# Metaformer block on one core: biases on a one in the input, moved tiles straight to the score rows, the opening re-ordered

## The reference, cut to what matters

```python
t = layernorm(x) @ W_prep + b_prep            # W_prep: 64 x (5*8*32): q_n, q, k, k_m, v
# wins: 32 windows, 64 tokens, 8 heads, 32 channels
bias, pat_n, pat_m = spatial(intrinsic)       # by relative position, 64 x 8 x 64 (x 32)
score = bias + einsum('bhod,ohid->bohi', q_n, pat_n)
score = score + einsum('bhod,bhid->bohi', q, k)
score = score + einsum('bhid,ohid->bohi', k_m, pat_m)
score = (score - mean_i) / std_i
x = x + einsum('bohi,bhid->bohd', score, v) @ W_fin + b_fin
x = x + experts(layernorm(x))                 # router, top 2 of 8, GELU, 64 -> 256 -> 64
```

## Time and profile before

| | |
|---|---|
| runs | 205.88 us median, 204.19 to 206.62 |
| profiled execution | 203.32 us, span of instructions 201.5 us |
| TensorE busy | 174.9 us (87%) |
| VectorE, ScalarE, GpSimd busy | 108.1, 117.9, 85.9 us |
| granted TensorE clock | 0.975 of full in the mean |
| DMA | 10868 packets, 12.96 MB |
| chain that ended last | TensorE 67%, GpSimd 14%, VectorE 8%, DMA 3% |

### The profile page before, as it was taken

One profiled execution on the slowest core, in us unless ns is written; L12 is line 12 of the kernel. 1 busy time (PEld: TensorE's weight loads), 2 busy tenths in 40 slices (PEclk: granted clock), 3 DMA queues, 4 the chain that ended last, 5 costly groups with the idle time before them and its releaser, 6 DMA issues.

```text
span 201.5 us, 4321 instructions
## 1 busy us (share of the span) xinstructions
PE 174.9 (87%) x1582; PEld 108.6 (54%) x1582; DVE 108.1 (54%) x296; ACT 117.9 (59%) x233; POOL 85.9 (43%) x130
## 2 busy tenths in 40 slices
PE   0519999999998799936995999999999999999983
PEld 0417554654555575626854856575556665655531
DVE  1594258445546525207386955196928773874323
ACT  2244397446453798808596497546666566676730
POOL 6120549040001999993866638481910073031000
PEclk9999999999999999985999789999999999999999
DMA  6930276969991002000300000000000000000000
GB/s 146 245 119 0 90 239 210 335 163 220 220 218 23 0 3 88 20 0 3 102 5 0 2 5 0 0 0 0 3 26 0 0 3 28 0 2 0 29 0 26
DMA packets 10868, 12.96 MB, mean 64 GB/s; under 512 B 2512, under 2 KB 8216, under 8 KB 10848
## 3 DMA queue, kind: packets, MB, share of 16 engines
q1 hardware_dynamic: 9936, 11.73, 22.2%
q10 hardware_dynamic: 528, 0.85, 1.5%
q0 software_dynamic: 384, 0.11, 0.5%
HBM read 7.94 MB, written 4.75 MB: 63 GB/s over the span
## 4 chain that ended last, share of the span: by engine, by line
PE 67%; POOL 14%; DVE 8%; DMA 3%; issue 3%; ACT 3%; SPq 1%; DVEq 0%; ACTq 0%; POOLq 0%
PE PS L731 13%; POOL SCN L437 10%; PE PS L571 9%; PE PS L719 7%; PE PS L720 6%; PE PS L805 4%; PE PS L585 4%; PE PS L780 4%; PE PS L595 3%; DMA XR<-in_x 3%; POOL RSC L455 3%; PE PS L628 2%; PE PS L604 2%; PE PS L769 2%; PE PS L698 1%
## 5 line engine op out<-in xcount | busy, mean ns | idle before, releaser
L938 ACT ACTIVATE HR<-PS,B1P 128x512 f32<-128x512 f32 x64 | 39.0, 693 | 5.0 <-PE PS L720 4.9
L731 PE MATMUL PS<-HR,W2s 128*64 128x512 f32 x128 | 31.0, 605 | 0.0
L437 POOL TENSOR_TENSOR SCN<-SCN,TMS 128x512 f32<-128x512 f32 x16 | 19.7, 1284 | 21.7 <-DVE SCN L1099 21.7
L719 PE MATMUL PS<-X,W1H 128*128 128x512 f32 x64 | 27.5, 430 | 0.0
L720 PE MATMUL PS<-X,W1L 128*128 128x512 f32 x64 | 25.8, 404 | 0.0
L443 POOL COPY PW<-PG 128x512 f32<-128x512 f32 x16 | 10.4, 684 | 34.1 <-DVE PG L1187 33.9
L1019 ACT ACTIVATE GB<-PS 128x512 f32<-128x512 f32 x16 | 9.6, 598 | 23.0 <-PE PS L805 23.0
L455 POOL TENSOR_TENSOR RSC<-VB,NHALF 128x32 f32<-128x32 f32 x4 | 21.9, 5463 | 0.3
L1158 DVE TENSOR_TENSOR SR<-PS,SCN 128x512 f32<-128x512 f32 x16 | 10.7, 685 | 13.6 <-PE PS L684 11.5
L974 ACT ACTIVATE BV<-PS 64x256 f32<-64x256 f32 x32 | 12.2, 380 | 7.6 <-PE PS L669 7.3
L731 PEld LDWEIGHTS PS<-HR,W2s 128*64 128x64 f32 x128 | 7.8, 136 | 13.3 <-issue 12.3
(11 more groups left out here) (149 smaller groups left out, 321.8 us busy)
## 6 DMA issues: line engine op xcount, KB each, us to landing
moved<-TMG SPq DMA_DIRECT2D x16, 256.0 KB, 2.9
TMS<-moved SPq DMA_DIRECT2D x16, 256.0 KB, 8.0
W1R<-in_W SPq DMA_DIRECT2D x4, 256.0 KB, 4.0
XR<-in_x SPq DMA_DIRECT2D x4, 128.0 KB, 4.7
W1E<-in_W SPq DMA_DIRECT2D x2, 256.0 KB, 6.2
W2s<-in_W SPq DMA_DIRECT2D x1, 512.0 KB, 3.7
out<-XR SPq DMA_DIRECT2D x4, 128.0 KB, 1.8
REL<-in_rel ACTq DMA_DIRECT2D x2, 225.0 KB, 5.1
```

The costliest lines, as they stand in the source:

```text
L437: G.tensor_tensor(pair, pair, TMS[:, t, :], ALU.add).then_inc(scn_ready, 1)
L719: nc.tensor.matmul(ps[:, :], W1H[:, col:col + P], X2[:, j * 512:j * 512 + 512], start=True, stop=False)
L731: m = nc.tensor.matmul(ps[d * C:d * C + C, :], W2s[:, 2 * (2 * ep + d) + c, :], HR[(4 * u + 2 * c + d) % 8][:, :], start=(c == 0), stop=(c ...
L938: A(HR[n % 8][:, :], PS[b][:, :], ACT.Gelu, bias=B1P[:, col:col + 1]).then_inc(bank_drained[b], 1)
```

## The change

- **Biases.** XF is stored as the transposed input plus one. The weights are centred over the 64 channels by a product with CEN (so that the one adds nothing), and b / 64 is added to each channel's weight by a first product of IDN with BPS (so that the one adds b; the normalised input sums to zero over channels). `bias_terms`, BI, YB, the DRAM tensor `bias_rows` and its DMAs go. The relative bias is added to the n table by SEL, with RB now on 4 x 2 rows in four DMAs.
- **Tiles of the m table.** SP sends each tile from TMG straight into SCN: two DMAs a tile, each with 128 source rows of 256 values and four target partitions, 32 in all. `moved`, TMS and GpSimd's additions go. VectorE adds the turned tiles of the n table to SCN in place, after a wait for all 32.
- **Order.** The n table is made before the transposes of XN. After the m tiles come all the keys and centred values, the experts' bias, and then the n tiles with their turned tiles alone. Keys and XC copies have no bias and are shared by ScalarE and VectorE. XN: two groups on VectorE, one on ScalarE, one on GpSimd. TensorE's first product waits for CEN and BPS, both from GpSimd. SP loads x 0, x 1, the weights and patterns; ScalarE's queue has b_prep, x 2 and x 3.
- **Buffers.** SQ has the place of TMS, and the opening's small tensors lie in it; TAM too.

The diff, cut:

```diff
-    plan += [(("xt", j), (4, 5, 7, 6)[j], 1) for j in range(NG)] + [(("wb",), 0, 1)]
+    plan += [(("tn", h), (4, 5, 7, 6)[h], 1) for h in range(4)]
+    plan += [(("xt", j), j, 1) for j in range(NG)]
     for m in range(8):
-        plan += [(("m", 2 * m + r), 4 + 2 * (m % 2) + r, 1) for r in range(2)]
-        if m == 1:
-            plan += [(("tn", h), h, 1) for h in range(4)]
+        plan += [(("m", 2 * m + r), 2 * (m % 2) + r, 1) for r in range(2)]
         if m == 3:
-            plan += [(("a", h), h, 1) for h in range(4)]
+            plan += [(("a", h), 4 + h, 1) for h in range(4)]
+    for m in range(8):
+        plan += [(("yk", 2 * m + r), 4 + 2 * (m % 2) + r, 1) for r in range(2)]
+        if m % 2 == 1:
+            plan += [(("xc", m // 2), m // 2, 1)]
+    plan += [(("b1", r), 4 + r, 1) for r in range(2)]
     for m in range(9):
         if m < 8:
-            plan += [(("n", 2 * m + r), r, 1) for r in range(2)]
-            plan += [(("yk", 2 * m + r), 4 + r, 1) for r in range(2)]
+            plan += [(("n", 2 * m + r), 4 * (m % 2) + r, 1) for r in range(2)]
         if m >= 1:
-            plan += [(("s", 2 * m - 2 + r), 2 + r, 1) for r in range(2)]
-        if m < 8 and m % 2 == 0:
-            plan += [(("xc", m // 2), 6, 1)]
-        if m == 1:
-            plan += [(("b1", r), 6 + r, 1) for r in range(2)]
...
-            for j in range(NG):
+            for j in range(2):
                 sp.dma_start(XR[:, 4 * j:4 * j + 4, :], x[:, 4 * j:4 * j + 4, :]).then_inc(x_in[j], 16)
-            sp.dma_start(BP[:, :], b_prep).then_inc(bp_in, 16)
-            sp.dma_start(B1[:, :], b1).then_inc(b1_in, 16)
+            sp.dma_start(WS[:, :], W_prep[:, 0:V * 256]).then_inc(wprep_in, 16)
+            sp.dma_start(REL[:, 1, :, :], rel[:, 1, :, :]).then_inc(relm_in, 16)
+            sp.dma_start(REL[:, 0, :, :], rel[:, 0, :, :]).then_inc(reln_in, 16)
+            for r in range(2):
+                sp.dma_start(WV[C * r:C * r + C, :], W_prep[:, V * 256:]).then_inc(wv_in, 16)
             for r in range(2):
...
             for tile in range(16):
                 sp.wait_ge(*drained("m", tile))
-                sp.dma_start(moved[P * tile:P * tile + P, :], TMG[:, tile, :]).then_inc(moved_out, 16)
-                if tile == 7:
-                    sp.wait_ge(bias_out, 16)
-                    load_bias(sp, 1)
-            sp.wait_ge(moved_out, 16 * 16)
-            rows = moved.rearrange("(i w) f -> i w f", w=NW)
-            for k in range(NPAIR // 2):
                 for g in range(2):
-                    sp.dma_start(TMS[C * g:C * g + C, 2 * k:2 * k + 2, :].rearrange("p t (b f) -> p (t b) f", b=2),
-                                 rows[:, 4 * k:4 * k + 4, 256 * g:256 * g + 256]).then_inc(moved_in[k], 16)
+                    tokens = SCN[C * g + 4 * tile:C * g + 4 * tile + 4, :, :, :, :]
+                    sp.dma_start(tokens.rearrange("p t b h o -> p (t b) (h o)"),
+                                 TMG[:, tile, 256 * g:256 * g + 256]).then_inc(moved_in, 16)
 
             sp.wait_ge(*filled("score", NPAIR // 2 - 1))
...
-            pool.dma_start(RB[:, :], rel0).then_inc(rel0_in, 16)
+            for h in range(4):
+                pool.dma_start(RB[HD * h:HD * h + 2, :], rel0.rearrange("(g h) r -> h g r", g=2)[h])\
+                    .then_inc(rel0_in, 16)
             for r in range(2):
                 pool.dma_start(LNB[C * r:C * r + C, :], ln_b).then_inc(lnb_in, 16)
...
+            G = nc.gpsimd
+            pool.wait_ge(consts_ready, 1)
...
+            pool.wait_ge(bp_in, 16)
+            G.tensor_scalar(BPS[:, :], BP[:, 0:SLOT], 1.0 / C, None, ALU.mult).then_inc(bps_ready, 1)
+            step(G.tensor_tensor(S2[:, :], IDN[:, 0:2], IDN[:, HD:HD + 2], ALU.add))
+            for h in range(2, 4):
+                step(G.tensor_tensor(S2[:, :], S2[:, :], IDN[:, HD * h:HD * h + 2], ALU.add))
+            G.tensor_scalar(SEL[:, :, :], S2[:, :].unsqueeze(2).to_broadcast([P, 2, P]), 1.0 / C, None,
+                            ALU.mult).then_inc(sel_ready, 1)
+            step(pool.memset(NHALF[:, :], -0.5))
+            pool.wait_ge(rx_ready, 1)
+            for q in range(12, NPAIR):
+                last = G.tensor_scalar(XN[:, q, :, :], twice(XR[:, q, :]), RS[:, q:q + 1], NB[:, q:q + 1],
+                                       ALU.mult, ALU.add)
+            last.then_inc(xn3_ready, 1)
...
-            pool.wait_ge(*drained("s", 14))
-            pool.wait_ge(*drained("s", 15))
-            for t in range(NPAIR):
-                if t % 2 == 0:
-                    pool.wait_ge(moved_in[t // 2], 32)
-                pair = SCN[:, t, :, :, :].rearrange("p b h o -> p (b h o)")
-                G.tensor_tensor(pair, pair, TMS[:, t, :], ALU.add).then_inc(scn_ready, 1)
 
...
+            def weights():
+
+                ps = begin("wt")
+                nc.tensor.matmul(ps[:, :], IDN[:, :], BPS[:, :].unsqueeze(2).to_broadcast([P, SLOT, C]),
+                                 start=True, stop=False)
+                for n_ in range(SLOT):
+                    m = nc.tensor.matmul(ps[:, n_ * C:n_ * C + C], WS[:, n_ * P:n_ * P + P], CEN[0:C, 0:C],
+                                         start=False, stop=(n_ == SLOT - 1))
+                end(m, "wt")
...
-            pe.wait_ge(consts_ready, 1)
+            pe.wait_ge(consts_ready, 2)
+            pe.wait_ge(bps_ready, 1)
             pe.wait_ge(wprep_in, 16)
...
+            weights()
             pe.wait_ge(relm_in, 16)
             pe.wait_ge(*drained("wt"))
             table("tm")
+            pe.wait_ge(reln_in, 16)
+            pe.wait_ge(rel0_in, 16 * 4)
+            pe.wait_ge(sel_ready, 1)
+            table("tn")
...
             for m in range(8):
                 pattern("m", m)
-                if m == 1:
-                    table("tn")
                 if m == 3:
                     products()
             for h in range(4):
+                pe.wait_ge(*drained("a", h))
+            for m in range(8):
+                mixed_keys(m)
+                if m % 2 == 1:
+                    centred(m // 2)
+            pe.wait_ge(w1e_in, 32)
+            pe.wait_ge(lnb_in, 32)
+            shift_bias()
+            for h in range(4):
                 pe.wait_ge(*drained("tn", h))
-                pe.wait_ge(*drained("a", h))
             for m in range(9):
                 if m < 8:
                     pattern("n", m)
-                    mixed_keys(m)
                 if m >= 1:
                     turned(2 * m - 2)
                     turned(2 * m - 1)
-                if m < 8 and m % 2 == 0:
-                    centred(m // 2)
-                if m == 1:
-                    pe.wait_ge(w1e_in, 32)
-                    pe.wait_ge(lnb_in, 32)
-                    shift_bias()
 
             def values(t):
                 ps = begin("v", t)
@@ -832,21 +788,19 @@
 
...
+                A(XF[:, 8 * j:8 * j + 8, :].rearrange("p w o -> p (w o)"), PS[b][:, :], ACT.Copy,
+                  bias=1.0).then_inc(bank_drained[b], 1)
...
+            dve.wait_ge(moved_in, N_MOVED)
+            for tile in range(16):
+                b = before[("s", tile)][0]
+                dve.wait_ge(*filled("s", tile))
+                part = SCN[:, :, :, :, 4 * tile:4 * tile + 4].rearrange("p t b h u -> p (t b) h u")
+                V_.tensor_tensor(part, PS[b][:, :].rearrange("p (h u w) -> p w h u", h=4, u=4), part,
+                                 ALU.add).then_inc(bank_drained[b], 1)
+            dve.wait_ge(*drained("s", 14))
+            dve.wait_ge(*drained("s", 15))
```

More of the change, by code:

```diff
@@ L202, in metaformer_kernel @@
         TMG = sb("TMG", [P, 16, 512])
[L204 to L219, removed]
+        WS = sb("WS", [C, 1024], at=sq_at)
+        WT_ = sb("WT_", [P, 4, 2, 2, C], at=sq_at)
+        REL = sb("REL", [P, 2, 2, NREL], at=sq_at)
+        RB = sb("RB", [P, NREL], at=sq_at)
+        TAM = sb("TAM", [P, SLOT, SIDE, SIDE], at=sq_at)
+        BPS = sb("BPS", [P, SLOT], at=sq_at)
+        VE = sb("VE", [P, NPAIR], at=sq_at)
+        RS = sb("RS", [P, NPAIR], at=sq_at)
+        RA = sb("RA", [P, NPAIR], at=sq_at)
+        BNX = sb("BNX", [P, NPAIR, 6], at=sq_at)
+        WARM = sb("WARM", [P, 1], at=sq_at)
+        NB = sb("NB", [P, NPAIR], at=sq_at)
+        assert sq_at[0] <= y_at[0]
+        PW = nc.alloc_sbuf_tensor_at("PW", [P, 4, 4, 2, C], F32, offset=scn_at[0])
         OR = sb("OR", [P, 8, 4, 2, HD + 1], at=late)
@@ L272, in metaformer_kernel @@
         small_in = sem("small_in")
[L273 to L276, removed]
+        moved_in = sem("moved_in")
         w1r_in = sem("w1r_in")
@@ L309, in metaformer_kernel, with twice @@
         N_SMALL = 9
[L311 to L315, removed]
-                queue.dma_start(BI[r0:r0 + WH, :, :], scratch[4 * g:4 * g + 4, :, lo:lo + WT]
-                                .rearrange("h j o -> j h o")).then_inc(bias_in[g], 16)
+        N_MOVED = 16 * 32
+        def twice(x):
```

(36 more changed lines are left out.)

157 lines of the change are left out of this document (39 added, 118 removed).

## The result

The changed kernel took 238.36 us in the median of four runs (236.47 to 241.26), the kernel before 206.25 on the same chip (204.19 to 208.25, four runs): ratio 1.151, 95% interval 1.134 to 1.167. It is slower, as forecast, but the forecast was 325 us; the profiled 236.47 us lie on the low end of the stated range (236), next to the third rival (246), which had set that end. Executions of one kernel can fall into two groups some 2 or 3% apart, so all ratios compare only the faster group of each kernel. The span of the profiled execution was 234.7 us.

A forecast was written before the change was run, and what follows sets the result against it. TensorE was taken to bound the kernel nearly throughout, with one break at GpSimd's 16 additions. Transfers done at 178.9 us, then 12.7, 3.4 for half clock and 130.4 after the last addition gave 325 us; range 236 to 341.

The forecast's parts named there:

- the third rival: Transfers to SCN: four engines drift apart to different partition groups, 55 GB/s, 76 us, 246 us in all; chance 0.25.
- The failed step: Transfers to SCN: priced from the bias_rows store out of eight partitions, 27 GB/s, 155 us for all 32.
- the 2.2 around a transfer: Transfers to SCN: 2.2 us added to their 155 us, from 2.9 to landing less 0.7 of moving.
- The argument used against drifting: Transfers to SCN: loads into 64 partitions also alternated between halves and stayed at 220 GB/s, so alternating didn't help.
- The rest of the sum: Whole kernel apart from moving the tiles: time is 170 us plus the transfers, once they outlast the cover.
- The opening: From the start to the m tiles: these begin at 19.7 instead of 21.26 us, a gain of 1.6 us.
- the 8.4 us expected from leaving out GpSimd's additions: Score stage: 6.4 us from an earlier RSC without TensorE's wait, plus 2.0 us from no half clock.
- no stall at RSC: Score stage: TensorE no longer waits at RSC, which ends at 84.1 instead of 90.8 us.
- the cover: TensorE work from the first transfer's issue at 21.7 to about 45 us, 23 us that can hide the transfers.
- the first: Rival for the transfers: several target groups fill at once, all hidden under 23 us, 191.6 us in all; chance 0.08.
- the second: Rival for the transfers: four engines each at full pace, 95 GB/s, 44 us, 214 us in all; chance 0.10.
- the fourth: Rival for the transfers: speed in proportion to partitions, 13.8 GB/s, 305 us, 475 us in all; chance 0.03.

The follow-up runs named there:

- m1: Only transfers of the changed kernel's shape, block not computed, in five series: 25 GB/s to one group of four partitions, 89 to 96 to partitions four apart.
- e1: Changed kernel with each transfer writing four partitions that lie four apart, in different groups; 225.22 us, ratio 1.121.
- e7: As e6, with the experts' bias products between the keys and the banks of the turned tiles exchanged; 216.76 us, ratio 1.057.
- e2: Changed kernel with the 32 transfers issued from GpSimd's queue instead of SP's; 249.01 us, ratio 1.238.
- e3: Changed kernel with the m tiles stored to DRAM and loaded back into SCN with 64 target partitions; 211.11 us, ratio 1.040.
- e5: Changed kernel with transfers from GpSimd's queue, each to four partitions of different groups; 216.08 us, ratio 1.045.
- e6: Changed kernel with transfers to four partitions of different groups, half issued by SP and half by GpSimd; 216.06 us, ratio 1.047.
- e8: Changed kernel with e7's two repairs and tiles over DRAM in two halves, loaded back by GpSimd's then SP's queue; 205.63 us beside 206.84 before.
- e9: As e8, with the DRAM tensor laid out so that loads read 8 KB rows and stores write 1 KB pieces; 207.92 us, ratio 1.016.
- e4: Changed kernel without the 32 transfers, SCN zeroed by GpSimd, so scores lack the m term; 199.9 us, ratio 0.974.
- f1: Kernel before, with SP sending the m tiles directly into TMS and nothing else changed; 247.71 us beside 206.84.
- f2: As f1, but GpSimd issues all loads of BI; 239.81 us, ratio 1.173.

## Why the prediction was right in its sign and wrong in its size

**The failed step** is the one that chose 27 GB/s, 155 us, for the transfers. The price itself was right for one group (25 measured, 26 at the start of the stretch), with some luck: it was read from a store to DRAM out of eight partitions, issued by GpSimd, and no run shows that the two have the same limit. To hold it for all 32 transfers was wrong. First issue to the end of the wait took 63.8 us, 61.6 without the 2.2 around a transfer: 68 GB/s in the mean. The engines drifted apart over different groups (m1, and the end packets in the changed kernel's own trace), and where nothing is shared the same shape has its full rate at once (e1). The argument used against drifting, that the loads into 64 partitions had alternated between halves and stayed at 220 GB/s, spoke about transfers with all 16 engines busy, each at 13.8 GB/s; it says nothing of four engines at one group, which have room to spread. Rival 3 had the mechanism, but took the loads' 13.8 GB/s for each drifted engine, 55 GB/s and 76 us; measured were up to 90, 22.5 an engine. That the time lies within the stated range is owed to this rival and not to the forecast's own step.

**The rest of the sum** was good to 5 us: 170.4 + 61.6 = 232.0 against 236.5. The difference, term by term:

- First issue at 23.05 instead of 21.7: +1.35. The first product started at 6.82 (6.9 forecast), but the weights took 5.7 us, not 3.6: the two passes of 512 columns took 2.04 us together, where I had 605 ns for one, and the 16 for centring 3.7 us, 0.23 us each and not 0.134. The opening gained 0.1 us.
- From the wait's end to the last addition 15.0 us, not 16.1: -1.1. The half clock after the wait was there.
- After the last addition 236.5 - 101.8 = 134.7 us, not 130.4: +4.3. Of the 8.4 us expected from leaving out GpSimd's additions 4.1 came. From the last addition to TensorE's first product after RSC it is 23.2 us, where before it was 92.25 - 64.5 = 27.75: 4.6 us and not 6.4, mostly since SR gained 0.7 us, not 2.0 (the bank, which e7 shows). The half clock behind the stall did go (1.00 from 125 to 132 us). But a later one grew: 0.51 for 7.0 us from 144 us on, behind 9 us in which TensorE was busy for 6.6, against this in the kernel before:

```profile
113.45:116.90 3.45, 3.45 (x16) 2.62 (x12) 2.26 (x8) 2.01 (x4) 0.63 (x1) 0.51 0.01 2
```

  That gives back 1.8 us, which leaves 0.7 of the 4.3 without a source. What sets the clock down there is open.

**Right:** the wait decides and stands ahead of the SCN additions; four engines; TensorE idle and then at half clock; no stall at RSC; the cover too short. **The rivals:** the first fell, and with it the 436 GB/s of the Trainium skill's Summary in "SBUF — State Buffer", which does not hold for four target partitions; the second (44 us) is nearly e1's rate, which the changed kernel reached only late; the fourth fell.

**The mechanism in all runs.** In every profile with the changed kernel's order the time is the end of VectorE's wait plus 149.0 to 149.7 us, wherever that end lies: 236.5 - 86.8, e1 225.0 - 75.3, e2 248.5 - 99.2, e3 209.4 - 60.1, e5 216.0 - 67.0, e6 216.1 - 66.7. With e7's two repairs it is 147 (e7, e8) and 148 (e9). So these runs missed their expectations in when the transfers ended, and e3 besides in the 2 us counted for the clock.

**Open:** the opening. In some profiles the m tiles began at 21.0 or 21.1 us (the changed kernel, e3, e6), in the others at 23.2 to 23.9. The same 16 transposes of XN took 1.97 us in the first and 3.4 to 3.7 in the others, with a granted clock of 1.00 in the rows of both. Which of the two an execution gets, and why, is not shown.

## What to carry to other kernels

Before a bounce over DRAM is taken out, count the partitions that each direct transfer writes at one time: here 4 MB sent four partitions at a time cost some 35 us, and the same bytes out to DRAM and back, staged in two halves, some 6 (e8 against e4, which sends nothing), enough to eat what the rest of the change gained. A rate read from one transfer is the price of a series only if all of the series meets at the same place; ask what changes from one to the next. And look at what stands behind a long wait in the same queue: small loads (f1) and fills (f2) wait with it.

## What the runs showed of the hardware that was not expected

- Four engines on one group of four partitions move 25 GB/s; in turn on two groups, they climb to 52; on neighbouring groups in turn to 70 (90 in the kernel, in twice as many transfers and in both halves of the partitions); on partitions four apart they have 89 to 96 at once. The end packets show the engines together in the first case and apart in the others that climb.
- The same transfers from GpSimd's queue keep 16 engines busy (share 1.09) at 69 GB/s in e2, and its issue number 32 waited 44.7 us (15.2 us in e5).
- TensorE's rows read a granted clock of 1.00 from 6 us on, and yet its first products were slow: 1.02 us for a pass of 512 columns against 0.605 later, and 0.23 us for each of L489's 16 passes of 64 columns, where 32 of 128 columns took 4.3 us, 0.134 each. Shapes differ there; the 16 transposes of XN, 1.97 or 3.67 us, are the same work.
